# Attention fused with FFN chunks: VectorE's and GpSimd's work in a fused step put in another order

## The reference

```python
x = x + 0.5 * ffn(layernorm(x))
x = x + attn(layernorm(x))
x = x + 0.5 * ffn(layernorm(x))
```

## Time and profile before

| what | value |
|---|---|
| median of 3 runs | 2206.65 us (2205.98 to 2212.32) |
| profiled execution, its own time | 2211.31 us |
| span in the trace | 2209.0 us |
| PE busy | 2143.3 us (97%) |
| PEld busy | 1972.8 us (89%) |
| DVE busy | 1433.1 us (65%) |
| ACT busy | 1034.0 us (47%) |
| POOL busy | 464.0 us (21%) |
| mean granted TensorE clock | 0.989 |

### The profile page before, as it was taken

How to read it: one execution, slowest core, us unless ns; L and a number is a source line. 1 busy time by engine, 2 the same in 40 slices (tenths; PEclk the granted TensorE clock), 3 DMA queues, 4 the chain that set the end, 5 groups by cost and what they waited for, 6 DMA issues and landing times. The chain is left out here.

```text
span 2209.0 us, 38336 instructions
## 1 busy us (share of the span) xinstructions
PE 2143.3 (97%) x14208; PEld 1972.8 (89%) x14208; DVE 1433.1 (65%) x3145; ACT 1034.0 (47%) x2004; POOL 464.0 (21%) x429
## 2 busy tenths in 40 slices
PE   7999999999999999999999899999999999999999
PEld 6888889999997798888888788888899999988887
DVE  6666546666665788888889897665466666633333
ACT  3333335555553666666666563333355555532222
POOL 2323211212121222222224332322111221200000
PEclk9999999999999999999999899999999999999999
DMA  9231225554454000000101101312234544441010
GB/s 274 99 99 56 73 64 138 135 138 102 101 118 133 20 6 15 20 20 1 34 1 49 44 11 56 119 63 73 61 90 108 116 100 101 112 131 58 30 58 20
DMA packets 194488, 168.38 MB, mean 76 GB/s; under 512 B 16905, under 2 KB 175037, under 8 KB 194304
## 3 DMA queue, kind: packets, MB, share of 16 engines
q1 hardware_dynamic: 176640, 144.57, 21.8%
q0 software_dynamic: 17664, 21.38, 5.5%
HBM read 104.32 MB, written 68.07 MB: 78 GB/s over the span
## 5 line engine op out<-in xcount | busy, mean ns | idle before, releaser
L328 PE MATMUL gate_up_p<-zh,w 128*128 128x512 f32 (+2 forms) x2368 | 708.9, 363 | 4.5 <-DVE zl L843 2.3
L650 ACT CAST hh<-h_s 128x512 fp32r<-128x512 f32 (+2 forms) x512 | 276.6, 540 | 709.2 <-DVE h_s L973 659.2
L366 PE MATMUL out_p<-w,hh 128*128 128x256 f32 x2816 | 567.1, 284 | 4.9 <-DVE hl L977 2.4
L328 PE MATMUL quad<-zh,w 128*128 128x512 f32 (+2 forms) x1728 | 483.1, 347 | 0.0
L328 PEld LDWEIGHTS gate_up_p<-zh,w 128*128 128x128 f32 x2368 | 431.6, 189 | 56.5 <-DVE h_s L973 2.8
L366 PEld LDWEIGHTS out_p<-w,hh 128*128 128x128 f32 x2816 | 464.0, 191 | 16.1 <-DVE hl L977 4.5
L328 PE MATMUL gate_up_p<-zl,w 128*128 128x512 f32 (+2 forms) x1184 | 423.8, 358 | 0.0
L366 PE MATMUL out_p<-w,hl 128*128 128x256 f32 x1408 | 396.9, 282 | 0.0
L973 DVE TENSOR_TENSOR h_s<-gate_up_p,sg_s 128x512 f32<-128x512 f32 (+2 forms) x296 | 178.7, 604 | 252.8 <-PE gate_up_p L328 223.4
L977 DVE TENSOR_TENSOR hl<-h_s,hh 128x512 fp32r<-128x512 f32 (+2 forms) x432 | 247.8, 574 | 136.8 <-ACT hh L650 116.0
L328 PEld LDWEIGHTS quad<-zh,w 128*128 128x128 f32 x1728 | 308.9, 188 | 27.2
(11 more groups left out here) (170 smaller groups left out, 2808.0 us busy)
## 6 DMA issues: line engine op xcount, KB each, us to landing
stage<-in_L_ffn_rg SPq DMA_DIRECT2D x128, 128.0 KB
stage<-in_L_ffn_ru SPq DMA_DIRECT2D x128, 128.0 KB
stage<-in_L_ffn_rd SPq DMA_DIRECT2D x128, 128.0 KB
slots_d<-empty SPq DMA_DIRECT2D x16, 662.5 KB, 7.7
zh_d<-zh SPq DMA_DIRECT2D x16, 512.0 KB
zl_d<-zl SPq DMA_DIRECT2D x16, 512.0 KB
y_d<-x SPq DMA_DIRECT2D x16, 512.0 KB
zh<-zh_d SPq DMA_DIRECT2D x16, 512.0 KB, 4.3
```

What stands on the lines that cost most here:

```text
L328: last = pe.matmul(dst, a, b, start=(k == 0), stop=(k == 3 * n - 1))
L366: last = pe.matmul(out[:, j // 2, o:o + C], a[:, par, cols], w[:, hi, :], start=(c == 0 and i == 0 and j % 2 == 0), stop=(c == NCH - 1 and ...
L650: nc.scalar.copy(hh[:, n % 2, 0:ncol], h_s[:, n % 2, 0:ncol]).then_inc(sm["hh_done"], 1)
```

## The change

What it does, part by part:

- On DVE `add_shared` stands behind the q/k normalisation and ahead of `h_product` n. At c = 0 `stats` stands behind the maximum (`highest`, cut off from `masked`), and `normal` behind `outputs`. `highest` stands behind `fused_low` n in all steps.
- `extras` is cut in `banks` (only what reads PSUM for `T`, `R` and `M`, late in the step, before `outputs`) and `others` (all else). `others(s - 1, 0)` stands where `extras(s - 1, 1)` was, `others(s - 1, 1)` ahead of `add_shared` and `h_product` n. So what belongs to chunk c of a step runs at the start of the next step, and what belongs to chunk c + 1 in its middle. `route3` is cut: the part that reads PSUM is in `banks`, `route_slots` in `others`.
- In `STEPS_OF`, `route4` of the first blocks is one chunk later, `var1` in one place with `var0`; the scatters are one step later.
- On PE `prep` for c stands between `gate` n + 1 and `up` n + 1, with the wait for `a_pl`, and only if there is something to prepare.
- On GpSimd the low parts of q and k stand ahead of the subtraction of the maximum, and `root` at c = 0 behind it.

```diff
--- before.py
+++ after.py
@@ -230,7 +230,9 @@
                           "route1": (0, 6), "route2": (0, 7), "M": (1, 0), "route3": (1, 0), "route4": (1, 1)}
         STEPS_OF[0][2].update(stats=(0, 5), var0=(0, 6), var1=(0, 7))
         for k in range(BEHIND + 1):
-            STEPS_OF[1][k].update(R=(k - 1, 4), route0=(k - 1, 5), route1=(k - 1, 6), route2=(k - 1, 7), M=(k, 0), route3=(k, 0), route4=(k, 1))
+            STEPS_OF[1][k].update(R=(k - 1, 4), route0=(k - 1, 5), route1=(k - 1, 6), route2=(k - 1, 7), M=(k, 0), route3=(k, 0), route4=(k, 2))
+        for k in range(BEHIND + 2):
+            STEPS_OF[1][k].update(var1=(k - 2, 4))
         XR_AT = {(NB - 1, 6): 0, (NB - 1, 7): 1}
         ROW_AT = {4: 0, 6: 1}
         PIECE_AT = [{(b, 6): b for b in range(NB)},
@@ -572,9 +574,10 @@
                     scores(keys, z, out)
                 loaded(f, phase, b, c + 1)
                 gate(n + 1, b % 2, c + 1, buf, SB)
+                if any(block_at(pf, step, pb, c) is not None for step in ("T", "R", "M")):
+                    wait(pe, sm["a_pl"], probs + 1 if probs is not None else upto(s, -LAG["probs"]))
+                    prep(pf, pb, c)
                 up(n + 1, b % 2, c + 1, buf, SB)
-                wait(pe, sm["a_pl"], probs + 1 if probs is not None else upto(s, -LAG["probs"]))
-                prep(pf, pb, c)
                 if probs is not None:
                     values(probs, keys, out)
                 if c == 0:
@@ -945,6 +948,8 @@
                 at = misc[:, 0, 0:BT * E].rearrange("p (e t) -> p t e", t=BT)
                 then(TS(over[:, :, :], at, float(CAP), FAR, ALU.is_ge, ALU.mult))
                 TT(pos[:, :, :], over[:, :, :], at, ALU.add).then_inc(sm["misc_free"], 1)
+
+            def route_slots(f, k):
                 dve.wait_ge(sm["misc_free"], use[(f, "M", k)] + 1)
                 then(TT(pos[:, :, :], pos[:, :, :], base[:, :, :], ALU.add))
                 for c in range(TOPK):
@@ -976,13 +981,22 @@
                 dve.wait_ge(sm["hh_done"], n + 1)
                 v.tensor_tensor(hl[:, n % 2, 0:ncol], h_s[:, n % 2, 0:ncol], hh[:, n % 2, 0:ncol], ALU.subtract).then_inc(sm["hl_done"], 1)
 
-            def prep(f, b, c):
-                for step, run in (("rows", ln_rows), ("T", prep_low), ("R", logits), ("route0", route0), ("route1", route1),
-                                  ("route2", route2), ("route3", route3), ("route4", route4),
-                                  ("stats", ln_stats), ("var0", ln_var0), ("var1", ln_var1)):
+            def prep_banks(f, b, c):
+                for step, run in (("T", prep_low), ("R", logits), ("M", route3)):
                     k = block_at(f, step, b, c)
                     if k is not None:
                         run(f, k)
+
+            def prep_others(f, b, c):
+                for step, run in (("route0", route0), ("route1", route1), ("route2", route2), ("route3", route_slots), ("route4", route4),
+                                  ("rows", ln_rows), ("stats", ln_stats), ("var0", ln_var0), ("var1", ln_var1)):
+                    k = block_at(f, step, b, c)
+                    if k is not None:
+                        run(f, k)
+
+            def prep(f, b, c):
+                prep_banks(f, b, c)
+                prep_others(f, b, c)
                 if (b, c) in XR_AT:
                     row_low(f, 0, XR_AT[(b, c)])
                     if XR_AT[(b, c)]:
@@ -1076,6 +1090,8 @@
                 wait(dve, sm["a_pt"], t)
                 v.tensor_tensor(p_s[:, :, :], quad[:, :, :].rearrange("p b (h c) -> p (b h) c", c=GROUP),
                                 causal[:, :].unsqueeze(1).broadcast_to([P, NH, GROUP]), ALU.add).then_inc(sm["a_masked"], 1)
+
+            def highest(t):
                 dve.wait_ge(sm["a_masked"], t + 1)
                 wait(dve, sm["a_sub0"], t)
                 v.tensor_reduce(smax[:, :], p_s[:, :, :], AX, ALU.max).then_inc(sm["a_max"], 1)
@@ -1105,9 +1121,14 @@
                 wait(dve, sm["a_yn"], t)
                 v.tensor_reduce(den_a[:, :], p_s[:, :, :], AX, ALU.add).then_inc(sm["a_den"], 1)
 
-            def extras(s, second):
+            def banks(s):
                 f, phase, b, c = fused_chunk(s)
-                prep(*prep_block(f, phase, b), c + second)
+                prep_banks(*prep_block(f, phase, b), c)
+
+            def others(s, second):
+                if s >= 0:
+                    f, phase, b, c = fused_chunk(s)
+                    prep_others(*prep_block(f, phase, b), c + second)
 
             def fused_step(s):
                 f, phase, b, c = fused_chunk(s)
@@ -1123,8 +1144,7 @@
                     v.tensor_tensor(azl[:, :, :], chunks(quad[:, 0, 0:C]), azh[:, :, :], ALU.subtract).then_inc(sm["a_zl"], 1)
                 if s == 0:
                     half_low(0, NEB - 1, NCH - 1)
-                else:
-                    extras(s - 1, 1)
+                others(s - 1, 0)
                 if ahead is not None and c:
                     normal(ahead)
                 if out is not None:
@@ -1142,28 +1162,32 @@
                     v.tensor_scalar(qke[:, :], ssq[:, :], 1.0 / C, RMS_EPS, ALU.mult, ALU.add).then_inc(sm["a_qke"], 1)
                     values_low(z)
                     qk_normal(z)
-                h_product(n, SB)
-                if probs is not None:
-                    dve.wait_ge(sm["a_ph"], probs + 1)
-                    v.tensor_tensor(pl[:, :, :], pairs, ph[:, :, :], ALU.subtract).then_inc(sm["a_pl"], 1)
+                others(s - 1, 1)
                 prev = before(phase, b) if phase == "s1" or b else ("s1", NB - 1)
                 if s == 0:
                     for j in range(ETILES[1]):
                         expert_row(0, NEB - 1, j)
                 elif c == 0:
                     add_shared(0 if prev[0] == "s1" else 1, *prev)
-                if ahead is not None and c == 0:
-                    stats(ahead)
-                    normal(ahead)
+                h_product(n, SB)
+                if probs is not None:
+                    dve.wait_ge(sm["a_ph"], probs + 1)
+                    v.tensor_tensor(pl[:, :, :], pairs, ph[:, :, :], ALU.subtract).then_inc(sm["a_pl"], 1)
                 if keys is not None:
                     masked(keys)
                 fused_low(n)
+                if keys is not None:
+                    highest(keys)
+                if ahead is not None and c == 0:
+                    stats(ahead)
                 h_product(n + 1, SB)
                 if keys is not None:
                     subtracted(keys)
-                extras(s, 0)
+                banks(s)
                 if probs is not None:
                     outputs(probs)
+                if ahead is not None and c == 0:
+                    normal(ahead)
                 fused_low(n + 1)
 
             def fused():
@@ -1176,7 +1200,8 @@
                     if s == LAG["z"]:
                         dve.wait_ge(sm["a_const"], 1)
                     fused_step(s)
-                extras(FSTEPS - 1, 1)
+                others(FSTEPS - 1, 0)
+                others(FSTEPS - 1, 1)
 
             v.memset(ones[:, :].bitcast(F32), 1.0)
             v.memset(mhalf[:, :], -0.5)
@@ -1268,18 +1293,18 @@
                     pool.wait_ge(sm["a_qke"], z + 1)
                     g.tensor_tensor(qkr[:, :], qke[:, :], mhalf[:, 0:2], ALU.pow).then_inc(sm["a_qr"], 1)
                 prep_fused(s)
-                if ahead is not None and c == 0:
-                    root(ahead)
-                if keys is not None:
-                    pool.wait_ge(sm["a_max"], keys + 1)
-                    g.tensor_tensor(p_s[:, 0:HALF, :], p_s[:, 0:HALF, :],
-                                    smax[:, 0:HALF].unsqueeze(2).broadcast_to([P, HALF, GROUP]), ALU.subtract).then_inc(sm["a_sub0"], 1)
                 if z is not None:
                     pool.wait_ge(sm["a_qc"], z + 1)
                     heads = lambda ap: ap.rearrange("p (h d) -> p h d", d=HD)
                     g.tensor_tensor(qcat[:, :, 2 * HD:3 * HD].bitcast(F32R), heads(qk[:, 0, :]), qcat[:, :, 0:HD], ALU.subtract)
                     g.tensor_tensor(kcat[:, :, HD:2 * HD].bitcast(F32R), heads(qk[:, 1, :]), kcat[:, :, 0:HD],
                                     ALU.subtract).then_inc(sm["a_qlo"], 1)
+                if keys is not None:
+                    pool.wait_ge(sm["a_max"], keys + 1)
+                    g.tensor_tensor(p_s[:, 0:HALF, :], p_s[:, 0:HALF, :],
+                                    smax[:, 0:HALF].unsqueeze(2).broadcast_to([P, HALF, GROUP]), ALU.subtract).then_inc(sm["a_sub0"], 1)
+                if ahead is not None and c == 0:
+                    root(ahead)
                 refill = c - 2 if phase == "s1" and b == NB - 1 else c + NCH - 2 if phase == "s0" and b == 0 else -1
                 if 0 <= refill < NCH:
                     piece_low(refill)
@@ -1314,9 +1339,9 @@
                         ln(1, k)
                     if at == first:
```

(4 more changed lines are left out.)

## The result

The changed kernel takes 2176.97 us (median of 4 runs, 2174.04 to 2181.53) against 2208.0 for the kernel before beside it: a ratio of 0.9859, 95% interval 0.9833 to 0.9885. That is 31 us less, where 22 were forecast. Measured once more in the experiments it was 2174.75 against 2207.92, ratio 0.9849 (0.9832 to 0.9865). The profiled executions differ by 36.2 us (spans 2209.0 and 2172.8): the one of before is 3.3 us over its median (2211.31) and the one of after 2.4 under its own (2174.56).

The account below looks back on a forecast made before the run. TensorE bounds the kernel, so only PE's waits can be won: 6.8 + 2.3 + 1.3 - 1.4 + 10 + 1.0 + 2 = 22.0 us off the profiled 2211.31, less 4.66 to the median: 2185, range 2174 to 2201.

Parts of the forecast that it names:

- the second rival: Whole kernel: clock stays up with every stall below 2 us, routing starts take all given; 34 us gained, 2173, chance 0.14.
- the head step: Fused step with c = 0, DVE adding a finished block: 20.96 to 19.6 us, new 1.6 us stall behind; 6.8 us gained.
- The clock: First twenty fused steps: PE's lowered clock after 2 us waits costs 4.6 us; 2.3 taken as gained, bounds 0 and 4.6.
- GpSimd's part: PE's waits on GpSimd's low parts of q and k: 1.3 us gained, one early wait before 752 included.
- GpSimd's order and the port: Low parts and `fused_low` take turns reading SBUF; DVE's subtraction ends 0.25 us later, costing 0.1 in 14 steps: -1.4 us.
- undisturbed steps: Fused steps bound by TensorE, 18.01 us with PE busy 17.79; forecast to take 18.0 to 18.1 after the change.
- the slack at the outputs is 0.57: Output sums end 0.57 us before PE asks for them, so a 0.25 us delay is nearly covered.
- The lock rival: `fused_low` and both low parts exclude each other in some 31 steps: 33 us lost against 22 gained, 2218, chance 0.07.
- Routing: Nine steps from 1133 to 1324: lost time falls from 29.3 to 19.3 us, 10 gained, bounds 4 and 17.
- The first routing step: Step at 1114: gives 1.0 us because its var0 leaves the end of the step before.
- The three last steps: Three steps behind the nine with routing, holding fewer stages: 2 of their 5.3 us of idle PE gained.
- Outside the fused stage ... nothing: Rest of the kernel: PE is never held by the order of the small DVE work, so nothing gained.

Follow-up runs that it names:

- the repeated run: The changed kernel measured again with no edit, beside the kernel before: 2174.75 us, ratio 0.9849.
- run 1: Not a label of its own: in "the repeated run 1 us" it is the unedited changed kernel measured again (2174.75 us), 1 us from the range's lower end.
- The stretched waits: Changed kernel plus an unread DVE reduction in each head step: 128x512 took 2190.06 us (ratio 0.9921), 128x1024 took 2193.91 us (0.9935).
- the run with the maximum first: Changed kernel with the maximum directly behind `masked` and `fused_low` behind it: 2169.37 us, ratio 0.9820 to the kernel before.
- the last run: Changed kernel with maximum directly behind `masked`, `gate` earlier on PE behind head steps, and shared add ahead of v's low part: 2181.84 us, ratio 0.9881.

## Why the prediction was right, and where it was off

**The number.** 2177 lies in the range, 3 us from its lower end (the repeated run 1 us), and nearer to the second rival's 2173 than to the 2185 that was forecast. Most terms of the sum came out too small and two too large; no single one hides the rest.

**Direction and main cause.** Right. The waits on the masked scores went, and a shorter wait behind the head step took their place, on the z transposes and behind the late normalisation, as said: 1.48 us where 1.6 was reckoned. A head step and the one behind it take 37.18 us; 19.6 + 18.0 had been said. Before it was 20.96 + 17.92 at full clock, so this is 1.7 us a block where the sum had 1.35.

**The clock** is the term that was mis-sized. "I take 2.3" of 4.6 in the first stretch, with both outcomes near this length: all of it came back, and the routing steps' part too (0.95 before, 1.00 after). Of 36.2 us of span 19.2 are busy time of PE. The stretched waits fit: at 1.5 us seldom a fall, at 2.1 in most cases. The prediction's second rival ("more comes back", 2173) had this right. That it was all of it in the profiled execution is in part luck: two other runs of the same kernel, at 0.997 and 0.998, took some 5 us more.

**Before the first full step.** 4.9 us were won there and 1.3 reckoned, for all of GpSimd's part. 0.9 of them lie ahead of the stage, in work that the change doesn't touch. Most of the rest belongs to a head step at 697 us that has no scores yet: there `fused_low` stood behind the add, the statistics and the normalisation, and PE waited 1.96 us for it. In the kernel before:

```profile
703.71 0.36 PE L366 MATMUL out_p<-w,hh 128*128 128x256 f32 x1 [1.96 <-DVE hl L1023]
...
703.71:717.77 14.06, 13.88 (x75) 12.12 (x75) 6.75 (x17) 5.81 (x16) 2.69 (x4) 0.88 0.00 0
```

Behind that wait the granted clock was 0.88 for 14 us, which makes up the 1.2 us that are left of the 4.1 won up to 717.77; the changed kernel has neither wait nor fall. The last 0.9 lie between 717 and 752 us. The walk began at the first scores and missed this head step.

**GpSimd's order and the port.** The mechanism was right, and close in its numbers. `fused_low` took 0.89 in undisturbed steps (between the 0.7 and 1.2 named), GpSimd's subtraction 1.04 (0.9 said), and DVE's subtraction ended 0.3 later (0.25 said). The step that failed is "the slack at the outputs is 0.57". That slack was measured in a step in which PE itself was held 0.2 to 0.4 us by the low parts. With that hold gone, PE arrives earlier and the slack is too small for the 0.3. PE's weight loads show it, at the transposes of q in the kernel before and at those of y in the changed one:

```profile
886.48 0.84 PEld L496 LDWEIGHTS misc<-ident,qcat 128*112 128x112 f32 x8 [0.40 <-POOL kcat L1281]
...
894.48 0.20 PEld L479 LDWEIGHTS quad<-ident,y_s 128*128 128x128 f32 x2 [0.25 <-DVE y_s L1117]
```

PE's own row beside the second has no wait, which is why its busy time reads 17.92 of 17.93. In the run with the maximum first the normalised sums are ready 0.17 us before PE wants them (892.84 against 893.01), and a step takes 17.63. So two terms were off in opposite ways: taking the hold away is worth up to 0.4 us a step (17.6 in the runs that have GpSimd's new order and the maximum directly behind `masked`), where I saw short gaps without a releaser, and the late maximum costs 0.3 of it. The sum, 18.01 to 17.93, hid both. The lock rival named the right instructions and the wrong size.

**Routing.** Nine steps lose 16.3 us to undisturbed length (178.43 - 162.1) where 19.3 were forecast, from 29.3: 13.0 gained for 10. Undoing the place gave 10.1 back there. The waits for pl ahead of `prep` were 0.2 to 0.6 us each and 1.0 in all, where 1.0 was said for M alone, and putting `prep` back made no difference to be seen. The first routing step, with the one before it, gave 0.2 (37.55 to 37.38) for the 1.0 that was said.

**The end.** The three last steps gave 0.7 where 2 were said. "Outside the fused stage ... nothing" was wrong by some 3 us in these two executions: between 1362 and 1530 us of the kernel before PE waits 0.7 us for a low part of h (L977) and 0.6 without a releaser, and the granted clock is 0.98 from 1460 to 1528 us; the changed kernel shows no wait there and 1.00. Whether the order of the preparation did that was not tested apart.

## What to carry to other kernels

Where one engine is the bound, look for the instructions of the others that stand between its releaser and the wait, and move them behind it; then ask what is late next, and expect the same chain to come up one wait later. A slack read in a step is only good as long as nothing else that holds the bounding engine in that step is taken away with it. Where VectorE and GpSimd work side by side, put the reduction, which was never held here, beside GpSimd's low parts, and the instruction with two SBUF inputs elsewhere (17.63 against 17.93 us a step).

## What the runs showed of the hardware that was not expected

Waits of TensorE of 1.9 us and more, one in each 75 us of otherwise full work, were followed by a lower granted clock in most cases, at 1.4 to 2.6 us each beyond the wait, and sometimes not at all at the same length (20.32 and 22.88 us for two steps with a wait of 2.43). Waits of 1.4 to 1.5 us mostly left it alone: none of six in the profiled changed kernel, but 20.50 instead of 19.00 us at 0.92 in one step of the last run with a wait of 1.37. Five us of added work so cost 15.3 by the medians.

Two DVE and GpSimd instructions that both read two SBUF tiles took turns even in short pieces: 0.68 became 0.89, and the GpSimd instruction behind it 1.19 instead of 0.74, while with the maximum first a reduction of 1.22 us ran beside that GpSimd instruction, and neither was held (1.22 and 0.74).

The Trainium skill (SBUF — State Buffer, Who interferes with whom) states it so: an instruction of VectorE with two SBUF inputs and one of GpSimd that reads SBUF exclude each other for a whole instruction, and a tensor_reduce is never held. These rows agree in both halves.
